# A vision tower on one core: where the sums and the normed rows of three norms are computed, and the engine that makes the ternary weights

## The reference, cut to what matters

```python
h = patches @ W.T + b                      # tok: 768 -> 256
x = concat([cls, h]) + pos_enc
# block 0, attention slot: gated recurrence over the tokens of an image
normed = (x - mu) * rsqrt(var + 1e-5) * gamma + beta
z = sigmoid(normed @ Wg.T + bg); c = normed @ Wc.T + bc
h_t = (1 - z_t) * h_{t-1} + z_t * c_t ;  x = h + x
# block 0, FFN: ternary weights
gamma = mean(|W|) + 1e-6
Wq = sign(W/gamma) * min(round(|W/gamma|), 1)          # -1, 0, 1
y = layernorm(gelu(x @ Wq_fc.T)) @ Wq_proj.T
# block 1: causal attention with rotary q, k (masked per image), then
# rows normed, scaled, clipped to +-127, rounded, times a ternary matrix
```

## Time and profile before

| what | us |
|---|---|
| median of three runs | 160.27 (159.31 to 160.37) |
| the profiled execution's own time | 159.69 |
| its span in the profile | 157.9 |

### The profile page before, as it was taken

How to read it: one execution, slowest core, us unless ns; L and a number is a source line. 1 busy time by engine, 2 the same in 40 slices (tenths; PEclk the granted TensorE clock), 3 DMA queues, 4 the chain that set the end, 5 groups by cost and what they waited for, 6 DMA issues and landing times.

```text
span 157.9 us, 3087 instructions
## 1 busy us (share of the span) xinstructions
PE 139.8 (89%) x874; PEld 111.3 (71%) x874; DVE 126.4 (80%) x404; ACT 96.0 (61%) x232; POOL 87.2 (55%) x159
## 2 busy tenths in 40 slices
PE   0599999999999996967996999789989989699993
PEld 0479898999889973545682757779878978596551
DVE  0031479989999998999996999699898979859893
ACT  3102288169264779999978785972476066368350
POOL 0000183455353657288995539989845786663530
PEclk9999999999999999999999999999999999869995
DMA  5999996000410000096595755797310000000243
GB/s 163 258 398 425 421 391 238 2 0 0 124 46 0 2 2 2 18 119 133 125 111 104 162 113 108 147 106 149 60 55 0 4 0 0 2 4 0 65 144 103
DMA packets 25621, 17.00 MB, mean 108 GB/s; under 512 B 20069, under 2 KB 23173, under 8 KB 25349
## 3 DMA queue, kind: packets, MB, share of 16 engines
q1 hardware_dynamic: 25605, 16.81, 40.3%
HBM read 9.70 MB, written 1.21 MB: 69 GB/s over the span
## 4 chain that ended last, share of the span: by engine, by line
DVE 26%; PE 22%; POOL 21%; issue 11%; ACT 8%; DMA 6%; SPq 4%; DVEq 0%; POOLq 0%; ACTq 0%
POOL small L1540 8%; DMA w_out_int<-w_out_in 6%; PE bank L661 5%; SPq L463 4%; POOL keys L1619 4%; POOL small L1535 4%; PE bank L758 3%; DVE stats L1093 3%; DVE gw L1414 3%; DVE gl L1106 2%; PE bank L832 2%; PE bank L792 2%; DVE rope L1460 2%; POOL small L1544 2%; POOL residual L1592 2%
## 5 line engine op out<-in xcount | busy, mean ns | idle before, releaser
L1540 POOL TENSOR_TENSOR small<-small,powers 128x1 f32<-128x1 f32 (+4 forms) x48 | 39.7, 826 | 6.0 <-DVE small L1403 2.8
L661 PE MATMUL bank<-w_tok,x_raw 128*128 128x256 f32 x108 | 27.7, 411 | 5.8 <-DMA w_tok<-w_tok_in 5.6
L661 PEld LDWEIGHTS bank<-w_tok,x_raw 128*128 128x128 f32 x108 | 21.5, 206 | 8.8 <-issue 5.6
L1535 POOL TENSOR_SCALAR small<-small 128x1 f32<-128x1 f32 x36 | 9.4, 260 | 24.9 <-DVE small L1101 23.2
L537 PE MATMUL bank<-pj,gt_hi 128*128 128x256 f16 x72 | 16.2, 273 | 0.7 <-issue 0.7
L537 PE MATMUL bank<-pj,gt_lo 128*128 128x256 f16 x72 | 16.2, 273 | 0.0
L932 ACT ACTIVATE n<-residual,small 128x256 f32<-128x256 f32 x18 | 10.7, 595 | 9.0 <-POOL small L1544 9.0
L537 PE MATMUL bank<-fc,n1t_hi 128*128 128x512 f16 x36 | 13.6, 379 | 0.6 <-ACT g L1002 0.3
L537 PE MATMUL bank<-fc,n1t_lo 128*128 128x512 f16 x36 | 13.6, 379 | 0.0
L1460 DVE SCALAR_TENSOR_TENSOR rope<-bank,packed,consts 128x324 f32<-128x324 f32 (+2 forms) x24 | 13.1, 608 | 0.3 <-POOL query L1613 0.2
L932 ACT ACTIVATE s<-end,small 108x256 f32<-108x256 f32 (+2 forms) x12 | 7.2, 596 | 9.4 <-POOL small L1544 6.2
(11 more groups left out here) (199 smaller groups left out, 411.7 us busy)
## 6 DMA issues: line engine op xcount, KB each, us to landing
x_raw<-x_in SPq DMA_DIRECT2D x9, 384.0 KB, 7.8
out_dram<-end SPq DMA_DIRECT2D x10, 108.0 KB
w_fc<-w_fc_in SPq DMA_DIRECT2D x1, 1024.0 KB, 10.0
w_pj<-w_pj_in SPq DMA_DIRECT2D x1, 1024.0 KB, 13.0
w_tok<-w_tok_in SPq DMA_DIRECT2D x2, 384.0 KB, 4.6
w_gate<-w_gate_in SPq DMA_DIRECT2D x1, 512.0 KB, 7.3
w_qk<-w_qk_in SPq DMA_DIRECT2D x1, 512.0 KB, 12.5
ln_w<-ln_w_in SPq DMA_DIRECT2D x1, 512.0 KB, 3.6
```

The lines of the kernel that those rows point to most:

```text
L661: mm(out[:, 0:D], x_raw[:, i, k, :], w_tok[:, k, :], start=(k == 0), stop=False)
L1535: return nc.gpsimd.tensor_scalar(small[0:n, i, out:out + 1], small[0:n, i, value:value + 1], factor, add, ALU.mult, ALU.add)
L1540: return gt(small[0:n, i, r:r + width], small[0:n, i, ve:ve + width], powers[0:n, 0:width], ALU.pow)
```

## The change

Five things are edited.

1. Sums. For norms 1, 2 and 3 `bn_stats` and `bn_aggr` go. The four VectorE instructions that write the rows (h1, proj, attend, c_row) also put out the sum of the row as accumulator (h1 becomes a scalar_tensor_tensor for it, c_row a tensor_scalar). ScalarE squares (sum - 256 x) over the 256 columns and accumulates it (steps sq1, sq2, sq3); its elementwise output goes to the slot of the normed tile and is overwritten. The sum of squares is 256 to the third times the variance, so GpSimd's scale gets the factor 1/256^3. VectorE makes the mean from the sum as one product of a column (steps mean1 to mean3, new meaning).
2. Normed rows. For all four norms GpSimd writes (x - mean) x r into the slot (steps n0, n1, n2, n3 of GpSimd), 9 + 9 + 9 + 12 instructions of 256 columns, instead of VectorE (norm 0) and ScalarE (norms 1 to 3). GpSimd's shifts for norms 1 to 3 go. VectorE keeps norm 0's statistics, its shift and r + 1 for the residual, which ScalarE still writes.
3. Ternary. w_below and w_ternary of VectorE go. ScalarE computes w / gamma + 1.5 x 2^23 in place (w_round, which rounds), then the sign of that minus 1.5 x 2^23 (w_sign), for fc and pj. VectorE's w_cut makes gamma and its reciprocal instead of the two cuts.
4. Two constants for it are set by memsets on VectorE (w_ones).
5. All four lists of `ORDER` are written anew, also for steps that are otherwise unchanged: on TensorE tok:5 now stands ahead of t0:0, and tok:8 behind gate:4 instead of ahead of gate:3; w_ln_bias moves behind h1:2.

```diff
+            def mean_of_sum(norm):
+
+                def stage(i):
+                    n = norm_rows(norm, i)
+                    dve.wait_ge(s[normed[norm][1]], i + 1)
+                    ts(col(i, MEANS[norm], 1, n), col(i, normed[norm][2], 1, n), 1.0 / D, None, ALU.mult)\
+                        .then_inc(s[f"mean{norm}_ready"], 1)
+                return stage
...
-                tt(res[:, i, :], narrow(("hs", i)), res[:, i, :], ALU.add).then_inc(s["h1_ready"], 1)
+                stt(out=res[:, i, :], in0=narrow(("hs", i)), scalar=1.0, in1=res[:, i, :], op0=ALU.mult, op1=ALU.add,
+                    accum_out=col(i, MV1)).then_inc(s["h1_ready"], 1)
...
-                    op0=ALU.mult, op1=ALU.add).then_inc(s["h2_ready"], 1)
+                    op0=ALU.mult, op1=ALU.add, accum_out=col(i, MV2)).then_inc(s["h2_ready"], 1)
...
+            def squares_of(norm):
+
+                def stage(i):
+                    h, ready, total, slot, free = summed[norm]
+                    n = end_rows(i) if norm == 3 else 128
+                    act.wait_ge(s[ready], i + 1)
+                    if i >= 2:
+                        act.wait_ge(s[free], i - 1)
+                    if i == 0 and norm == 2:
+                        act.wait_ge(s["pe_fold"], KD)
+                    if i == 0 and norm == 3:
+                        act.wait_ge(s["pe_gate"], 4 * CHUNKS)
+                    go(slot[0:n, i % 2, :], h[0:n, i, :], ACT.Square, bias=small[0:n, i, total:total + 1], scale=-float(D),
+                       accum_out=small[0:n, i, total + 1:total + 2]).then_inc(s[f"mv{norm}_ready"], 1)
+                return stage
...
+            def w_round(n):
+
+                _, w, _ = ternary[n]
+                act.wait_ge(s["cut_ready"], 2)
+                act.wait_ge(s["round_ready"], 2)
+                go(w[:, :, :], w[:, :, :], ACT.Identity, scale=derived[:, D_INV_GAMMA + n:D_INV_GAMMA + n + 1],
+                   bias=derived[:, D_ROUND:D_ROUND + 1]).then_inc(s["rounded_ready"], 1)
+
+            def w_sign(n):
+                out, w, ready = ternary[n]
+                act.wait_ge(s["rounded_ready"], n + 1)
+                go(out[:, :, :], w[:, :, :], ACT.Sign, bias=derived[:, D_ROUND + 1:D_ROUND + 2]).then_inc(s[ready], 1)
...
-            def shift(i, nb, mv, r, ready, n=128):
-
-                nc.gpsimd.tensor_scalar(small[0:n, i, nb:nb + 1], small[0:n, i, mv:mv + 1],
-                                        small[0:n, i, r:r + 1], -1.0, ALU.mult, ALU.mult).then_inc(s[ready], 1)
+            def applied(out, h, i, mv, r, n=128):
+
+                return nc.gpsimd.tensor_scalar(out, h[0:n, i, :], small[0:n, i, mv:mv + 1], small[0:n, i, r:r + 1],
+                                               ALU.subtract, ALU.mult)
...
+            def n1_(i):
                 pool.wait_ge(s["r1_ready"], i + 1)
-                shift(i, NB1, MV1, R1, "nb1_ready")
+                if i >= 2:
+                    pool.wait_ge(s["pe_t1"], i - 1)
+                pool.wait_ge(s["mean1_ready"], i + 1)
+                applied(n1[:, i % 2, :], res, i, NB1, R1).then_inc(s["n1_ready"], 1)
```

The first pieces are VectorE's mean and two of its sums, then ScalarE's squares and the ternary, last GpSimd's application (n0, n2 and n3 are alike). The steps n1, n2 and n3 of ScalarE go whole. The new orders around the steps that the prediction speaks of, ScalarE's and GpSimd's:

```diff
+        w_sel:0 h0:0 h0:1 w_abs_fc:0 h0:2 w_gate:0 h0:3 n0:0 w_abs_pj:0 w_abs_ln:0 h0:4 c_t0:0 n0:1 t0:0 h0:5 t0:1
+        t0:2 w_round:0 w_qk:0 t0:3 h0:6 t0:4 w_round:1 n0:2 h0:7 n0:3 n0:4 gate:0 t0:5 w_ln_b:0 gate:1 w_sign:0
+        gate:2 h0:8 t0:6 w_sign:1 n0:5 t0:7 w_fold:0 sq1:0 t0:8 sq1:1 gate:3 n0:6 w_ln_w:0 sq1:2 w_fold:1 gate:4
...
+        w_tok:0 h0:0 n0:0 c_pow:0 h0:1 h0:2 h0:3 n0:1 n0:2 n0:3 h0:4 n0:4 w_ln:0 h0:5 n0:5 h0:6 n0:6 h0:7 n0:7 h0:8
+        n0:8 h1:0 h1:1 n1:0 hc:0 n1:1 hc:1 h1:2 n1:2 h1:3 hc:2 n1:3 hc:3 h1:4 c_pow:1 n1:4 h1:5 n1:5 square:0 h1:6
+        n1:6 square:1 h1:7 c_pow:2 hc:4 n1:7 square:2 h1:8 proj:0 n1:8 n2:0 hc:5 proj:1 c_pow:3 proj:2 square:3 n2:1
```

More of the change, by code:

```diff
@@ L1326, in c_row @@
                 dve.wait_ge(s["pe_gate"], 4 * CHUNKS)
[L1327 removed]
+                ts(end[0:IMAGES, 0, :], narrow(("c_row", 0), IMAGES), 1.0, 0.0, ALU.mult, ALU.add,
+                   accum_out=col(0, MV3, 1, IMAGES)).then_inc(s["h3_ready"], 1)
             def shift(i, nb, mv, r, ready):
```

219 lines of the change are left out of this document (104 added, 115 removed).

## The result

| | before | after |
|---|---|---|
| median (range) of 4 runs, us | 160.32 (159.31 to 160.80) | 169.92 (169.76 to 171.77) |
| ratio | | 1.068, 95% interval 1.061 to 1.075 |
| span of the profiled execution, us | 157.9 | 168.0 |

What follows compares the result with a forecast made beforehand. No engine alone was taken to bound the kernel; the chain's owner changes by stage. Terms -3.6, +0.8, +1.9 and -2.0 made -2.9 us on 159.69, so 156.8, or 157.4 as median; range 153.5 to 163.5.

Steps and rivals of the forecast that it cites:

- the price in one term: GpSimd's 256-column application taken as 0.60 us; 39 of them less 30 shifts made +12.1 us of GpSimd time.
- +1.9: Shifts on the old chain, 2% or about 3.2 us, become GpSimd applications at 0.60 for 0.378 us: +1.9 us.
- (c): 60 to 115 us: GpSimd becomes the bound, eight longer applications plus holds beside gw or gl; 163.1 us, chance 0.13.
- First stage 0, last stage 0: No gain or loss in the first stage or the last, where TensorE is busy 18.66 of 20 us.
- statistics -3.6: VectorE's statistics, 3% of the chain or 4.7 us; 30 of 39 leave it: -3.6 us.
- reads +0.8: Some ten VectorE accumulator reads come onto the chain: +0.8 us.
- TensorE's waits -2.0: Of TensorE's 2.5 us waiting for normed rows from ScalarE, 2.0 us go.
- Squares: ScalarE's 30 squares over 256 columns: 0.50 us plus 0.198 for the accumulator read, 0.70 each.
- Rounding and sign: ScalarE's ternary over 2048 columns, 28 to 47 us: rounding 2.11, sign 2.00, twice 4.11 = 8.2 us, costed at 0.
- (d): 29 to 60 us: ScalarE's four long ternary instructions delay TensorE, two uncovered; +4.1 us, 161.5, chance 0.11.
- (e): Sign is not in sigmoid's table, so four further ScalarE table loads between gates; +5.1 us, 162.5, chance 0.03.
- The port: Shared SBUF port: VectorE's gw and gl could stand behind GpSimd applications, up to 18 x 0.6 us; leaned to the slower rival.

Runs made afterwards that it cites:

- The probe: Kernel before with eight instructions, among them application, tensor_tensor and copy, tried one after another on GpSimd in its idle first 15 us: 160.3 us in total.
- 90 columns: Kernel after with each of GpSimd's 39 applications writing only the first 90 of 256 columns, queue orders untouched: 157.0 us, ratio 0.982.
- six relocations: Six variants of the kernel after with applications, whole or in part, moved from GpSimd to VectorE or ScalarE queues: 165.6 to 169.6 us.

## Why the prediction was wrong

**The step that failed is the price in one term: "Size and type are those of the latter and only one input is missing, so I take 0.60."** The application costs 1.23 us undisturbed and 1.32 in the mean of the 39 (51.3 us). Both bounds, 0.378 and 0.728, were rows of other operations: the lower a tensor_scalar on one column, the upper a tensor_tensor on 256. The upper was taken for an upper end because it reads one input more. The probe shows that this does not order GpSimd's operations: the tensor_tensor took 0.61 and the tensor_scalar 1.22 on the same tile. There was no row of a wide tensor_scalar on GpSimd, and so no upper end at all; the range should have said so. With 51.3 us for the 39 the term is 51.3 - 30 x 0.378 = +40.0 us and not +12.1, and GpSimd as a whole went up by 37.9, to 125.1 us, where the forecast had 99.

**The price alone does not mend the sum.** The forecast gave the shifts 2% of the old chain, 3.2 us, which is eight or nine of them. At 1.32 us each these make a term of +7.9 for +1.9, and a time of 163.4: 6.5 us short of 169.9. So the count failed too: after, line 1559 holds 15% of 168.0 us on the chain, 25 us or some nineteen applications. And some 4 us go with TensorE's lower clock, for which the forecast had no term. A term that is a share of the old chain holds only while the chain stays where it was; here the step became over three times as long, and the chain moved to it.

**The rival was named and priced too low.** (c), GpSimd becomes the bound from 60 to 115 us, had 0.13 and 163.1, with "It decides from the point where an application costs over 0.7 with its holds; above about 1.0 the gain is gone". The sign given for it, an application of 0.9 us in the mean, is passed by far. But the price was taken only for eight shifts on the chain between 60 and 115 us. The runs show it biting outside that stretch too: about half of it at norm 3, where (c) had nothing, with the lower clock of TensorE that goes with it. The forecast's "First stage 0, last stage 0 (TensorE holds 18.66 of 20)" looked at what held the last stage before the change and not at what 12 applications of twice the length would do to it: groups of norm 3 come from GpSimd every 2.4 to 2.7 us (152.28, 154.69, 157.40 and 159.97 in the timeline of the kernel after).

**The rest of the sum held, as a whole.** With the application at 0.69 us, 0.79 in the mean, the time was 157.0 for a forecast of 157.4. In part that is luck: by the forecast's own term an application of 0.79 makes +3.5 for +1.9 and 159.0, so something else was worth 2 us more than forecast. The stage from the first gelu to the last did become shorter, as the forecast wanted for a sign: 39.6 us before, 37.2 after, 35.6 at 90 columns. Whether each term (statistics -3.6, reads +0.8, TensorE's waits -2.0) is right is not shown. The parts alone, in the old order and with the applications still on ScalarE, each cost time.

**Term by term.** Squares 0.505 + 0.193 for 0.70: right. Rounding and sign 2.08 and 2.03 for 2.11 and 2.00, hidden in the new order (the first gelu begins at 60.2 us, 59.7 before; with 90 columns 58.7): right, and (d) falls in the new order. In the old order the ternary alone cost 1.3%, in the range that the expectation gave to (d); whether by its place or otherwise was not isolated. (e) falls: four table loads. h1's new form 0.421 for 0.475: too dear by 0.5 us in all. ScalarE 104.8 for about 107. VectorE 113.3 for 106.6: 1.9 us is the held clip, 0.7 gw and gl; for the rest, durations of VectorE's rows overlap their neighbours' (before, they sum to 152.1 us where the engine is busy 126.4), so that taking out instructions by their full length takes out too much. The port, by the Trainium skill (SBUF — State Buffer, Who interferes with whom) as an estimate up to 18 x 0.6 us on gw and gl: in the means gw rose from 1.276 to 1.299 us and gl from 1.222 to 1.277, 0.7 us for all 18. The same section of the Trainium skill says that whoever issues first decides. The one clip that stood behind GpSimd for 1.9 us agrees in so far as a GpSimd instruction was under way when it began; that it then stood behind two more, which began after it, the sentence does not give.

## What to carry to other kernels

A bound taken from another operation bounds nothing: before a wide operation moves to an engine on which no row shows it, time it there by itself, in idle time of the kernel at hand. A cost in a kernel whose queues are fixed by hand is best tested by changing a duration and no queue; the 90-column run settled in one go what six relocations could not. A term that is read as a share of the chain before is good for small changes of length only; where a step grows by a factor, work out how many times it will stand on the new chain. And a part that is tried alone is tried with the load that the other parts would have moved: here the squares alone met a ScalarE that still had the applications.

## What was not expected of the hardware

- GpSimd's tensor_scalar with a subtraction and a product: 1.22 us on 128x256 f32, 3.3 to 3.4 ns a column, twice its tensor_tensor (0.61) and three times its copy (0.40); 32, 72 and 108 rows take no less time than 128 (1.217, 1.302, 1.227).
- GpSimd's tensor_tensor with one input a column broadcast over 256 costs no more than with two full inputs (0.61 both).
- TensorE was busy 1.95 us of the three before 154 us; from there on the granted clock stood at 0.50 while it was busy 3.00 of 3 us, and an output unit took 1.08 us instead of 0.65. In the kernel before, 1.91 us of 3 came ahead of a stretch at 0.55. What the fall wants was not tried.
- VectorE's 32-row clip, with one input, begun while a GpSimd application was ending and 0.05 us ahead of two GpSimd sums with two inputs each, took 2.34 us and ended 0.14 us behind them. At 90 columns it took 0.43 us, and the next one, begun inside two such sums, 1.19.
